# Narrow attentions: later query products and the output product from three fp16 products of split parts in place of fp32

## What is computed

```python
# L0, with k = v = ctx and q = layernorm(x)
kp = k @ Wk.T + bk
qp = q @ Wq.T + bq
att = einsum('bhqd,bhkd->bhqk', qh, kh) * scale
...
# L3
q = (Q @ Wq + bq).reshape(b, sq, H, DHEAD).transpose(0, 2, 1, 3)
k = (K @ Wk + bk).reshape(b, -1, H, DHEAD).transpose(0, 2, 1, 3)
v = (V @ Wv + bv).reshape(b, -1, H, DHEAD).transpose(0, 2, 1, 3)
scores = jnp.where(m == 0, -jnp.inf, einsum('bhqd,bhkd->bhqk', q, k) / sqrt(DHEAD))
out = einsum('bhqk,bhkd->bhqd', softmax(scores), v)
return out.transpose(0, 2, 1, 3).reshape(b, sq, DM) @ Wo + bo
```

## Time and profile before

| | |
|---|---|
| median of 3 runs | 2559.26 us (2558.38 to 2561.86) |
| span of the profiled execution, its own time | 2560.1 us |
| TensorE busy | 2184.1 us, 85% |
| VectorE, ScalarE, GpSimd busy | 61%, 55%, 38% |
| mean granted TensorE clock | 0.919 of full speed |
| the two narrow attentions | about 255 and 283 us |

### The profile page before, as it was taken

How to read it: one execution, slowest core, us unless ns; L and a number is a source line. 1 busy time by engine, 2 the same in 40 slices (tenths; PEclk the granted TensorE clock), 3 DMA queues, 4 the chain that set the end, 5 groups by cost and what they waited for, 6 DMA issues and landing times. The chain is left out here.

```text
span 2560.1 us, 62725 instructions
## 1 busy us (share of the span) xinstructions
PE 2184.1 (85%) x23986; PEld 1476.7 (58%) x23986; DVE 1558.2 (61%) x3640; ACT 1411.1 (55%) x2999; POOL 964.7 (38%) x1069
## 2 busy tenths in 40 slices
PE   5898489599999999958789999999984993899846
PEld 2565346367777777745546666666652561566634
DVE  3666583476566556636767777777764744555464
ACT  2666563365555555524466666666663652566644
POOL 3543132154454445404423333333333742433135
PEclk8999699799999999968889999999996995999968
DMA  5664271300000000010200000000013224432034
GB/s 121 116 116 78 88 240 41 121 20 14 14 8 14 14 14 2 2 34 1 82 14 15 14 9 15 14 15 9 2 40 109 93 65 116 103 75 69 22 114 126
DMA packets 118581, 139.59 MB, mean 55 GB/s; under 512 B 15072, under 2 KB 107184, under 8 KB 118288
## 3 DMA queue, kind: packets, MB, share of 16 engines
q1 hardware_dynamic: 110900, 115.39, 17.5%
q0 software_dynamic: 7392, 20.19, 2.6%
HBM read 93.25 MB, written 17.47 MB: 43 GB/s over the span
## 5 line engine op out<-in xcount | busy, mean ns | idle before, releaser
L952 DVE TENSOR_REDUCE a_mx<-a_pair 112x2 f32<-112x750 f32 x256 | 238.1, 937 | 198.3 <-PE a_pair L1021 198.3
L1260 POOL TENSOR_TENSOR a_kp<-a_kp 125x512 f16<-125x512 f32 x192 | 217.6, 1158 | 259.3 <-ACT a_kp L1351 259.3
L353 POOL TENSOR_SCALAR a_P<-a_P,a_inv 112x375 f32<-112x375 f32 x256 | 148.9, 595 | 378.0 <-DVE a_inv L484 377.0
L890 ACT ACTIVATE a_PT<-a_pair 125x672 f32<-125x672 f32 x256 | 186.3, 731 | 70.2 <-PE a_pair L1033 65.6
L391 ACT ACTIVATE a_P<-a_masked,a_least 112x375 f32<-112x375 f32 x256 | 153.4, 600 | 83.5 <-DVE a_least L479 81.7
L1394 DVE SCALAR_TENSOR_TENSOR a_k<-a_p,a_k 128x375 f16<-128x375 f32 x128 | 69.3, 547 | 139.1 <-ACT a_k L1307 139.1
L1351 ACT CAST a_kp<-a_kp 125x512 f16<-125x512 f32 x192 | 110.3, 616 | 76.9 <-DVE a_kp L1413 76.9
L572 PE MATMUL a_p<-a_kc,a_wk 128*128 128x375 f16 x768 | 147.0, 327 | 4.3 <-POOL a_kc L347 4.3
L1493 PE MATMUL a_p<-a_kc,a_wk 128*128 128x375 f16 x768 | 142.2, 326 | 6.3 <-POOL a_kc L1252 6.3
L479 DVE CUSTOM_DVE_ANT_0 a_masked<-a_s,a_mask_add 112x375 f32<-112x375 f32 x256 | 129.9, 546 | 27.1 <-PE a_s L609 26.1
L586 PE MATMUL a_p<-a_wv,a_kc 128*125 128x512 f16 x576 | 141.9, 383 | 5.2 <-DVE a_v L518 3.6
(11 more groups left out here) (447 smaller groups left out, 5352.8 us busy)
## 6 DMA issues: line engine op xcount, KB each, us to landing
a_kc<-in_ctxT SPq DMA_DIRECT2D x64, 375.0 KB, 3.3
a_k<-a_k_parts SPq DMA_DIRECT2D x192, 93.8 KB
w_stage<-in_L_ffn_W SPq DMA_DIRECT2D x32, 512.0 KB, 5.8
w_stage<-in_L_ffn_ew SPq DMA_DIRECT2D x16, 512.0 KB, 6.1
w_stage<-expert_rows SPq DMA_DIRECT2D x16, 448.0 KB, 7.7
a_v_in_sb<-in_ctx SPq DMA_DIRECT2D x16, 375.0 KB
a_q<-a_q_parts SPq DMA_DIRECT2D x48, 112.0 KB, 3.8
w_stage<-in_L_ffn_W SPq DMA_DIRECT2D x16, 256.0 KB, 4.0
```

The costliest lines, as they stand in the source:

```text
L353: pool.tensor_scalar(P[:, p % 4, r, :], P[:, p % 4, r, :], inv[:, p % 4, r:r + 1], 1.0, ALU.mult, ALU.mult).then_inc(P_done, 1)
L890: act.activation(PT[:, p % 4, :, :], pair_bank[slot["turned", p]][0:KP, :, 0:KT * S], ACT.Exp).then_inc(exp_done, 1)
L952: dve.tensor_reduce(mx[:, b % 2, 2 * pair:2 * pair + 2], pair_bank[slot["score", p]][0:S, :, 0:SK], AX.X, ALU.max).then_inc(max_done, 1)
L1260: pool.tensor_tensor(kp16[:, LO, j, hf, r, :, :].rearrange("p c m -> p (c m)"), kp[:, n % 4, :], kp16[:, HI, j, hf, r, :, :].rearrange("p ...
```

## The change

- Query products of groups 1 to 3 (steps 3 and later) are made of six fp16 matmuls of split parts, `wq16` by `x16`, in place of two fp32 ones. Group 0 stays as it was.
- The output product is made of six fp16 matmuls, `yT16` by `wo16`.
- `wq16` and `wo16` are made once a phase: ScalarE's high part (`high_weight`), VectorE's low part (`low_weight`), in steps -10 and -6.
- `x16` for a group's 448 columns in both chunks (896 elements a partition) is made in step 32g - 31 (1, 33, 65): ScalarE `high_x`, VectorE `low_x`. Both come last in their engine's step.
- The turned output is emptied in two stages: ScalarE writes the high part (`y_hi`), then VectorE reads the same bank and writes the low part (`low_yT`), and only this one counts up `emptied`.
- The scale 1/64 goes into ScalarE's evacuation of the queries and into `add_out`, which becomes a multiply and add.

```diff
+    SPLIT_AT = (-10, -6)
...
+                        if kind == "q" and b >= 1:
+                            by = by / WS
...
-                        act.copy(yT[:, :, :], p_bank[:, 0:DC * S].rearrange("p (c s) -> p c s", s=S)).then_inc(emptied, 1)
+                        act.copy(yT16[:, HI, :, :], p_bank[:, 0:DC * S].rearrange("p (c s) -> p c s", s=S)).then_inc(y_hi, 1)
+
+                def high_weight(i):
+                    act.mul((wq16, wo16)[i][:, HI, :, :], (wq, wo)[i][:, :, :], WS).then_inc(qo_hi, 1)
+
+                def high_x(g):
+                    if g >= 2:
+                        act.wait_ge(projected, number["q", g - 1, 1] + 1)
+                    act.copy(x16[:, HI, :, :], XT[:, :, g * GW:(g + 1) * GW]).then_inc(x_hi, 1)
...
+                    if s in SPLIT_AT:
+                        high_weight(SPLIT_AT.index(s))
+                    for g in range(1, G):
+                        if s == 32 * g - 31:
+                            high_x(g)
...
-                    dve.tensor_tensor(X[:, b, :], p_bank[0:S, 0:D], X[:, b, :], ALU.add).then_inc(emptied, 1)
+                    dve.scalar_tensor_tensor(X[:, b, :], p_bank[0:S, 0:D], 1.0 / WS, X[:, b, :], ALU.mult,
+                                             ALU.add).then_inc(emptied, 1)
+
+                def low_yT(b):
+                    dve.wait_ge(y_hi, b + 1)
+                    dve.tensor_tensor(yT16[:, LO, :, :], p_bank[:, 0:DC * S].rearrange("p (c s) -> p c s", s=S),
+                                      yT16[:, HI, :, :], ALU.subtract).then_inc(emptied, 1)
+
+                def low_weight(i):
+                    dve.wait_ge(qo_hi, i + 1)
+                    w16, w = (wq16, wo16)[i], (wq, wo)[i]
+                    dve.scalar_tensor_tensor(w16[:, LO, :, :], w[:, :, :], WS, w16[:, HI, :, :], ALU.mult,
+                                             ALU.subtract).then_inc(qo_split, 1)
+
+                def low_x(g):
+                    dve.wait_ge(x_hi, g)
+                    dve.tensor_tensor(x16[:, LO, :, :], XT[:, :, g * GW:(g + 1) * GW], x16[:, HI, :, :],
+                                      ALU.subtract).then_inc(x_split, 1)
...
+                        if kind == "turn_n":
+                            low_yT(b)
                         if kind == "out":
                             add_out(b)
+                    if s in SPLIT_AT:
+                        low_weight(SPLIT_AT.index(s))
+                    for g in range(1, G):
+                        if s == 32 * g - 31:
+                            low_x(g)
...
+                    elif kind == "q" and b >= 1:
+                        pe.wait_ge(qo_split, 1)
+                        pe.wait_ge(x_split, b)
+                        for n, (x, z) in enumerate(PARTS):
+                            for i in range(DC):
+                                mm = pe.matmul(p_bank[:, 0:GW], wq16[:, z, i, c * 128:(c + 1) * 128], x16[:, x, i, :],
                                                start=n == i == 0, stop=(n, i) == (2, DC - 1))
...
-                        for i in range(DC):
-                            mm = pe.matmul(p_bank[0:S, 0:D], yT[:, i, :], wo[:, i, :], start=i == 0, stop=i == DC - 1)
+                        pe.wait_ge(qo_split, 2)
+                        for n, (x, z) in enumerate(PARTS):
+                            for i in range(DC):
+                                mm = pe.matmul(p_bank[0:S, 0:D], yT16[:, x, i, :], wo16[:, z, i, :],
+                                               start=n == i == 0, stop=(n, i) == (2, DC - 1))
```

More of the change, by code:

```diff
@@ L701, in narrow_attention_phase @@
         wk16 = m.sb("wk16", [128, 2, DC, D], F16)
+        wq16 = m.sb("wq16", [128, 2, DC, D], F16)
+        wo16 = m.sb("wo16", [128, 2, DC, D], F16)
         const = m.sb("const", [2, GW], F16)
@@ L720, in narrow_attention_phase @@
         w_hi, w_split, kc_hi, kc_split = (m.sem(n) for n in ("w_hi", "w_split", "kc_hi", "kc_split"))
+        qo_hi, qo_split, x_hi, x_split, y_hi = (m.sem(n) for n in ("qo_hi", "qo_split", "x_hi", "x_split", "y_hi"))
         kc_in = [m.sem(f"kc_in{i}") for i in range(3)]
@@ L784, in narrow_attention_phase @@
         yn = m.sb("yn", [S, 2, D])
-        yT = m.sb("yT", [128, DC, S])
+        yT16 = m.sb("yT16", [128, 2, DC, S], F16)
+        x16 = m.sb("x16", [128, 2, DC, GW], F16)
         two_banks = lambda name: m.stack.enter_context(nc.psum_tensor(f"{tag}_{name}", [128, 2, 512], F32))
```

## The result

The changed kernel takes 2579.18 us (median of 4 runs, 2577.05 to 2580.69), the kernel before 2558.82 us beside it (2554.99 to 2561.86): a ratio of 1.0075, 95% interval 1.0062 to 1.0088. By the ratio it is some 19 us slower, by the two medians 20.4. The profiled execution of the changed kernel spans 2576.3 us.

What follows compares the result with a forecast made beforehand. TensorE's own instructions were taken to set the pace. The terms -4.6 - 7.9 + 14.0 + 9.4 + 3.7 + 5.0 = +19.6 us on the profiled 2560.1, less 0.8 for the median, gave about 2579 us; range 2563 to 2591.

Steps and rivals of the forecast that it cites:

- Queries: Query products of groups 1 to 3: each 0.46 us shorter on TensorE, ten counted, -4.6 us.
- Output: Output products: 0.72 us in place of 1.05 on TensorE, 24 of 32 counted, -7.9 us.
- The hand-over: p_bank freed 0.5 us later after the turned output; 22 key-product waits, four later maxima, two phase ends: +14.0 us.
- Late maxima: From batch 11 on, the next maximum starts 0.5 us later while TensorE waits: some four times, 2.0 us.
- The split for groups 2 and 3: Steps 33 and 65, both phases: low_x delays the next maximum, TensorE stalls ahead of turned scores, 4 x 2.35 = +9.4 us.
- The clock: Half clock follows two of the four 2.4 us TensorE gaps, costing 2.5 us each: +5.0 us.
- The split for group 1: Step 1, each phase: the first changed query product ends 1.1 to 2.2 us later, 2 x 1.85 = +3.7 us.
- Weight splits: Steps -10 and -6, where VectorE is free and ScalarE waits: cost nothing, at most 0.3 us each.
- the waits stay short: Rival: VectorE finds slots, key products and turned scores wait no longer, only savings remain: some 2547 us; chance 0.07.
- Only the XT split hides: Rival: the turned output's bank wait stays but low_x costs nothing: +1.5 us, about 2561 us; chance 0.11.
- The maxima's DMA waits go: Rival: the first attention's five waits on maxima transfers and their half clock, some 18.6 us, vanish: 2560 us; chance 0.06.
- The stalls grow: Rival: GpSimd's copy gets in first, half clock follows all four gaps, or a maxima wait joins: 2586 to 2592; chance 0.16.

Runs made afterwards that it cites:

- the move to GpSimd: Changed kernel with the turned output emptied once by ScalarE in fp32 and split by GpSimd: 1.0052 of before; with x16 also made in the lead-in, 0.9970.
- GpSimd out of the way: Changed kernel with GpSimd's bias addition and copy of values one step earlier: 1.0059 of the kernel before.
- the queries alone: Changed kernel with only the query products from split parts, output product and its emptying as before the change: 1.0079 of the kernel before, +20 us.
- the kernel with only group 1 late: Changed kernel with x16 for groups 2 and 3 made in the lead-in, group 1 still in step 1: 1.0029 of the kernel before.
- the kernel with XT split ahead: Changed kernel with x16 for all three groups made in the lead-in (step -26): 0.9996 of the kernel before.
- the first four variants: The first four edited kernels, run as one set on one chip; before's own median beside them was 2559.9 us. The text does not list them.

## Why the prediction was right

Predicted 2579 us, measured 2579.18, well inside the range. The mechanism holds: both kinds of wait are where they were said to be, with the releasers named. That the sum hits to the microsecond is luck: the terms did not all hit, they made up for one another, and one that was left out moved too. Point by point:

- **Queries.** 0.46 us a product, and the periods show 0.46. Right.
- **Output.** Predicted 0.72 us a product, measured 0.79, about what the value products of the same width take (0.80); the saving is 0.26, not 0.33. By the 24 products counted that is 6.2 us, not 7.9. The estimate took the low end of its bounds of 0.68 and 0.78, and the measured value lies just above them.
- **The hand-over.** Predicted 0.5 us in each of 22 places; measured 0.35 to 0.40 idle in the trace and 0.43 by the period, with its releaser the one named. VectorE's half took 0.390 us as estimated. Late maxima: 1.08 in place of 0.71, the ends 0.86 in place of 0.43. So 9.5 + 1.5 + 0.9 = 11.9 us, not 14.0; in the last attention alone the move to GpSimd (with XT ahead in both) shortens the phase by 5.6 us, and twice that is 11.2.
- **The split for groups 2 and 3.** Four stalls, at the named place, by the named releaser. Predicted 2.35 us each, measured 2.72, 2.72, 1.95 and 1.95: 9.3 us against 9.4. The evenness was wrong, and that the sum agrees is luck. In the first attention GpSimd's plain copy got in first too, by which the sum was to be higher; so the Trainium skill's rule ("SBUF — State Buffer", "Who interferes with whom") stands here with its number, 2.22 us for an instruction that takes 1.09 alone. In the last attention the conflict with the bias addition cost what was reckoned: low_x, ready at 2251.61, ended 1.46 us later, against 1.45 in the working. The stall is shorter there because low_x and the maximum behind it ended some 0.2 us earlier than laid out, the output product ended 0.07 us later, and the bracket counts from the modelled end of the score product, 0.17 us behind the time at which the turned scores could have followed. By the prediction's own measure, start against start, the stalls are 2.88 and 2.12 us.
- **The clock.** Two of four stalls were to be followed by the half clock; all four were, even those of 1.95 us, but the loss behind each is nearer 1.5 us than 2.5: 19.92 less 16.45 is 3.47 us, of which 1.95 is the stall. Some 6 us against 5.0. The cost of one stretch and the count were both off, in opposite directions. And the step under the count does not hold: the prediction went by the length of the gap. Of the stalls of 1.58 us with GpSimd out of the way two were followed by the half clock and two were not, and the stall of 2.07 us with the queries alone was not. So four of four is no rule, and what decides it is open.
- **The split for group 1.** Predicted +3.7 us over before. The product starts 2.25 us later in the chain, as worked out (2.3), though the 1.85 us a phase of the sum lies above the mean of its own 1.1 and 2.2. In the last attention's lead-in 50.8 us against 48.5 (the kernel with only group 1 late), so 2.3 us a phase, and 4.6 for two; the means over all profiles give 5.0. The changed kernel's own lead-in there took 48.8 us, so single lead-ins differ by as much as the term.
- **Weight splits.** 0.69 us each on VectorE with no wait behind them: nothing, as said.

With these the sum is -4.6 - 6.2 + 11.9 + 9.3 + 6 + 4.6 = +21 us, against +19.6 predicted and about +19 measured. The waits on the maxima's DMA were taken as unchanged; they were 15.3 us in place of 11.1 in the profiles. That they differ as much between kernels with the same queues says that this is not shown to be the change's doing.

The two profiled executions are 16.2 us apart. From its first turned scores to its last addition to x the first attention takes 9.9 us more than before, the last one 6.7 more; the stretches from the first query product to the first turned scores take 1.6 and 0.3 more, and all else together 2.3 less. The last attention has no DMA waits on the maxima; by the terms above it should lose 7.4 us, near the 6.7. Of the first attention's 9.9 us, 4.2 are those DMA waits. The 5.7 left are fewer than the 9.0 that the terms give there. So a part of the agreement with +19.6 rests on waits that the prediction took as unchanged.

Of the rivals, "the waits stay short" fell: both waits are there. "Only the XT split hides" is not what the change does, but it is what the kernel with XT split ahead does: 0.9996, where the rival's price was +1.5 us, 0.06%. "The maxima's DMA waits go" did not happen. "The stalls grow" happened in part: the copy got in first, all four stalls were followed by the half clock, and the DMA waits of that profile are 4.2 us longer, though at fewer places (four in place of five); the total stayed below its 2586 because the other terms came out smaller.

What is not settled: what sets the landing of the maxima in the first attention, and so what of the first attention's excess in the run of the queries alone is chance; and what brings the half clock behind a stall of 1.6 to 2.1 us.

## What to carry to other kernels

Shorter products are worth what they take off the pace-setting engine only if the making of their operands stays out of its waits. Here 11 us of savings came with 32 us of waits and half clock, from instructions that themselves take 0.4 and 1.1 us, and making the same parts at other places turned 0.75% slower into 0.3% faster. Before an engine with free time is given a further instruction, look at what is queued behind it and who waits for that. A bank that is handed through two engines is one instruction longer for all who share it: empty it once, and split from the copy.

## What was not expected of the hardware

- A VectorE instruction on small tensors, 0.17 us, took 1.03 us beside a GpSimd copy, though it has one tensor input. The conflict is not only that of two-tensor instructions.
- The length of a stall did not tell whether the half clock would follow. In the changed kernel stalls of 1.95 us were followed by half-clock products (2.16 us against 1.31), and one of 1.58 us was too with GpSimd out of the way; another of 1.58 us, one of 2.07 us, and the gap of 1.41 us of the earlier trace rows were not.
- The same kernel before took 2558.8 to 2573.4 us in the medians of different sets (the three sets of the variants ran on three chips), more than most of the effects in this study. The profiles show where: from the last attention's last addition to x to the end of the span, a stretch that no kernel here changes, it is 122 to 125 us in the six profiles of the first kernels (before, the change and the first four variants) and 136 to 140 us in the seven of the two later sets. Only ratios within a set carry.
